# Residual with a matrix per subject on one core: the subjects' numbers and the weights loaded by another engine, in other row counts

## The chip, the cores and the metric

One core of a Trainium2 chip runs the whole program. The metric is the device time of one execution in microseconds; three executions of the kernel before gave 323.35, 324.01 and 324.10 us (median 324.01).

## The reference

There are 128 samples of 128 x 1024 f32 (`x`, indices b, c, t), a number 0 to 7 for each sample (`subjects`) and 8 matrices of 128 x 128 f32 (`weights`). The output is the input plus a product with the sample's own matrix:

```python
w = weights[subjects]
out = x + jnp.einsum('bct,bcd->bdt', x, w)
```

So 64 MB are read, 64 MB written, and each sample takes one 128 x 128 by 128 x 1024 product in f32.

## The kernel before, in words

A tile is two samples, one on partitions 0 to 63 and one on 64 to 127; each partition holds two neighbouring rows of a sample (8 KB). There are 64 tiles. Tiles travel in pairs: one load brings two tiles (2 MB). `x_ring` has 12 slots, so room for 6 pairs, and a result is written over its own input before it is stored from there.

SP (line 88 on) issues the load of the weights first (line 90: 128 partitions, 4 KB each in four pieces of 1 KB), then the 32 loads of x (line 98). The loads of pairs 4 and 5 wait for the landing of pairs 0 and 1. From pair 6 on each load waits until everything stored from its slots has landed (`x_out`, line 95). ACT (line 171 on) issues the load of the subjects' numbers, the same 128 numbers on 16 partitions (line 190), although only partition 0 is read, and all stores (lines 202 and 205): single tiles for the first two and the last four, pairs for the rest. Thus there are two hardware queues in use, and the order inside each is the program's order. Nothing but `x_ring`'s slots ties loads to stores.

Before the first product, DVE clamps the subjects' numbers (line 144). Then DVE and ACT wait for the weights and rearrange them into `weight_bank` (lines 113 and 174), each two copies of 64 x 1024. POOL has made an identity (`eye`, lines 102 and 106), which DVE adds (line 119), so that the product brings part of the residual with it. DVE loads numbers into registers (line 124) and copies the matrices of four tiles into `weight_ring` (line 132, "pick"). TensorE then does 16 matmuls and 16 weight loads per tile (line 222); DVE adds x to two quarters of the products (lines 139 and 140), ACT copies the other two (lines 182 and 183), and ACT issues the store.

Of the kernel before, what the change touches and what calls it, by code (L numbers as in the profile page):

```python
# [6 lines left out]
DMA_INC = 16  # L7
# [7 lines left out]
def subject_residual_kernel(nc, x, subjects, weights, out):  # L15
# [9 lines left out]
    f32, i32 = mybir.dt.float32, mybir.dt.int32  # L25
    B, C, T = x.shape
    S, _, D = weights.shape
    assert C == D == nc.NUM_PARTITIONS
    H, R = C // 2, 2
# [6 lines left out]

    SINGLE = (*range(PAIR), *range(TILES - REST, TILES))

    SUBJECT_ROWS = 16

    def stores(pairs, place):

        return sum(PAIR if (pair * PAIR_SLOTS + place) * PAIR in SINGLE else 1 for pair in range(pairs))
# [3 lines left out]
    EVENS, ODDS = slice(0, S, 2), slice(1, S, 2)  # L47
    add = mybir.AluOpType.add

    x_of_pair = x.rearrange("(n j a) (h r) t -> n (a h) j (r t)", j=PAIR, a=2, r=R)  # L50
    out_of_pair = out.rearrange("(n j a) (h r) t -> n (a h) j (r t)", j=PAIR, a=2, r=R)

    with ExitStack() as ctx:  # L53
        x_ring = ctx.enter_context(nc.sbuf_tensor("x_ring", [C, SLOTS, R, T], f32))

        weight_halves = ctx.enter_context(nc.sbuf_tensor("weight_halves", [C, S // 2, R, D], f32))
# [3 lines left out]

        eye = ctx.enter_context(nc.sbuf_tensor("eye", [C, H], f32))
        subject_row = ctx.enter_context(nc.sbuf_tensor("subject_row", [SUBJECT_ROWS, B], i32))
        product = [[ctx.enter_context(nc.psum_tensor(f"product{i}_{a}", [D, T], f32)) for a in range(2)]
                   for i in range(PRODUCTS)]

        subjects_in = ctx.enter_context(nc.semaphore("subjects_in"))
        clamped = ctx.enter_context(nc.semaphore("clamped"))
        weights_in = ctx.enter_context(nc.semaphore("weights_in"))
        eye_zero = ctx.enter_context(nc.semaphore("eye_zero"))
        eye_low = ctx.enter_context(nc.semaphore("eye_low"))  # L70
        eye_high = ctx.enter_context(nc.semaphore("eye_high"))
# [15 lines left out]

        @block.sync
        def _(sp):
            sp.dma_start(weight_halves[:, :, :, :],  # L90
                         weights.rearrange("(i a) (h r) d -> (a h) i (r d)", a=2, r=R)).then_inc(weights_in, DMA_INC)
            for pair in range(PAIRS):
                lap, place = divmod(pair, PAIR_SLOTS)
                if lap:
                    sp.wait_ge(x_out[place], stores(lap, place) * DMA_INC)
                elif place >= LOADS_AHEAD:
                    sp.wait_ge(x_in[place - LOADS_AHEAD], DMA_INC)
                sp.dma_start(x_ring[:, place * PAIR:(place + 1) * PAIR, :, :], x_of_pair[pair]).then_inc(x_in[place], DMA_INC)

        @block.gpsimd  # L100
        def _(pool):
            pool.memset(eye[:, :], 0.0).then_inc(eye_zero, 1)  # L102
            pool.wait_ge(eye_zero, 1)
            for begin, made in ((0, eye_low), (H, eye_high)):
                half = slice(begin, begin + H)
                pool.affine_select(eye[half, :], eye[half, :], pattern=[[-1, H]], base=0, channel_multiplier=1,  # L106
                                   compare_op=mybir.AluOpType.not_equal, fill=1.0).then_inc(made, 1)

        @block.vector
        def _(dve):  # L110
            def bank(half, source, subjects_of):

                return dve.tensor_copy(  # L113
                    weight_bank[half, subjects_of, :, :].rearrange("h i r (q k) -> h i r q k", q=2),
                    weight_halves[source, :, :, :].rearrange("h i r (k q) -> h i r q k", q=2))

            def add_eye(half, row, columns):
                cells = weight_bank[half, :, row, columns]
                return dve.tensor_tensor(cells, cells, eye[half, :].rearrange("h (s k) -> h s k", s=1).broadcast_to(  # L119
                    (H, S, H)), add)  # L120

            def subjects_of(tile):

                _, numbers = nc.values_load_multi_w_load_instructions(  # L124
                    subject_row[0:1, tile * 2:(tile + PICK_AHEAD) * 2], engines=(mybir.EngineType.DVE,), min_val=0,
                    max_val=S - 1, skip_runtime_bounds_check_because="DVE has clamped subject_row to 0 .. S - 1")
                return numbers

            def pick(slot, numbers):

                for subject, half in zip(numbers, (LOW, HIGH)):
                    done = dve.tensor_copy(weight_ring[half, slot, :, :], weight_bank[half, bass.ds(subject, 1), :, :])  # L132
                return done

            def sums(tile, slot):

                low, high = product[slot % PRODUCTS]
                dve.wait_ge(multiplied, tile + 1)
                dve.tensor_tensor(x_ring[LOW, slot, 0, :], low[LOW, :], x_ring[LOW, slot, 0, :], add)  # L139
                dve.tensor_tensor(x_ring[HIGH, slot, 1, :], high[HIGH, :], x_ring[HIGH, slot, 1, :], add).then_inc(summed, 1)  # L140

            dve.sem_inc(summed, PRODUCTS)
            dve.wait_ge(subjects_in, DMA_INC)
            dve.tensor_scalar(subject_row[0:1, :], subject_row[0:1, :], 0, S - 1, mybir.AluOpType.max,  # L144
                              mybir.AluOpType.min).then_inc(clamped, 1)
            dve.wait_ge(weights_in, DMA_INC)
            bank(LOW, LOW, EVENS)
            bank(LOW, HIGH, ODDS).then_inc(bank_low, 1)
            dve.wait_ge(eye_low, 1)
            dve.wait_ge(bank_low, 1)  # L150
            add_eye(LOW, 1, ODD)
            dve.wait_ge(eye_high, 1)
            dve.wait_ge(bank_high, 1)  # L153
            add_eye(HIGH, 0, EVEN).then_inc(eyes_added, 1)
            dve.wait_ge(eyes_added, 1)
            dve.wait_ge(clamped, 1)
            numbers = subjects_of(0)
            for tile in range(PICK_AHEAD):
                pick(tile, numbers[tile * 2:tile * 2 + 2]).then_inc(picked, 1)


            for tile in range(TILES):
                sums(tile, tile % SLOTS)
                ahead = tile + PICK_AHEAD
                if ahead < TILES:
                    if ahead % PICK_AHEAD == 0:
                        numbers = subjects_of(ahead)
                    own = ahead % PICK_AHEAD * 2
                    pick(ahead % SLOTS, numbers[own:own + 2])

        @block.scalar
        def _(act):
            def bank(half, source, subjects_of):
                return act.copy(  # L174
                    weight_bank[half, subjects_of, :, :].rearrange("h i r (q k) -> h i r q k", q=2),
                    weight_halves[source, :, :, :].rearrange("h i r (k q) -> h i r q k", q=2))

            def cross(tile, slot):

                low, high = product[slot % PRODUCTS]  # L180
                act.wait_ge(multiplied, tile + 1)
                act.copy(x_ring[LOW, slot, 1, :], low[HIGH, :])  # L182
                act.copy(x_ring[HIGH, slot, 0, :], high[LOW, :]).then_inc(copied, 1)  # L183

            def whole(tile):

                act.wait_ge(copied, tile + (PRODUCTS + 1))
                act.wait_ge(summed, tile + (PRODUCTS + 1))  # L188

            act.dma_start(subject_row[:, :], subjects.rearrange("(one b) -> one b", one=1).broadcast_to(  # L190
                (SUBJECT_ROWS, B))).then_inc(subjects_in, DMA_INC)
            act.sem_inc(copied, PRODUCTS)
            act.wait_ge(weights_in, DMA_INC)
            bank(HIGH, LOW, EVENS)
            bank(HIGH, HIGH, ODDS).then_inc(bank_high, 1)
            for tile in range(TILES):
                slot = tile % SLOTS
                place, j = divmod(slot, PAIR)
                cross(tile, slot)
                if tile in SINGLE:  # L200
                    whole(tile)
                    act.dma_start(out_of_pair[tile // PAIR, :, j, :], x_ring[:, slot, :, :]).then_inc(x_out[place], DMA_INC)
                elif j == PAIR - 1:
                    whole(tile)
                    act.dma_start(out_of_pair[tile // PAIR], x_ring[:, place * PAIR:(place + 1) * PAIR, :, :]).then_inc(
                        x_out[place], DMA_INC)
            for place in reversed(range(PAIR_SLOTS)):
                act.wait_ge(x_out[place], DMA_INC * stores(LAPS + (place < REST // PAIR), place))
# [39 lines left out]
```

## Time and profile before

| What | before |
|---|---|
| span of the profiled execution | 321.5 us |
| time of that same execution | 323.31 us (1.8 us lie outside the span) |
| median of three executions | 324.01 us |
| data moved | 134.83 MB, mean 419 GB/s over the span |
| PE / DVE / ACT / POOL busy | 76% / 61% / 41% / 0% |
| queue q1 (SP's), queue q10 (ACT's) | 50.2% and 49.4% of the 16 DMA engines' span |

How to read it: "DMA share" is the mean busy share of the 16 DMA engines. Packets are booked at rounded durations, so a full stretch can read 1.01. A share of 0.31 means that about 5 of 16 engines have work. A landing time runs from the issue of a transfer to the moment at which all of it has arrived.

### The profile page before, as it was taken

To read this page: it belongs to the slowest core of one execution; us is meant where nothing else is said; L and a number is where in the kernel's file an instruction comes from. 1 tells how busy PE (TensorE), PEld (TensorE's weight loads), DVE (VectorE), ACT (ScalarE), POOL (GpSimd) and SP (SyncE) were. 2 spreads that over 40 slices of the span, in tenths; PEclk is the share of its full clock that TensorE was granted. 3 is DMA by queue.
4 is the path that set the end of the run, shared out by engine and by line. 5 is a ranking of instruction groups with operands and counts; after the bars stand their busy time and mean duration, and the time that the engine had idled before them with its cause. 6 is when DMAs were issued, how large, how long until landed. Compare 5 with 4: busy or idle time off the path is not lost.

```text
span 321.5 us, 2871 instructions
## 1 busy us (share of the span) xinstructions
PE 243.8 (76%) x1024; PEld 112.7 (35%) x1024; DVE 196.3 (61%) x261; ACT 132.2 (41%) x131; POOL 0.8 (0%) x7
## 2 busy tenths in 40 slices
PE   0799997878687866779868698666986868876650
PEld 0344442334343432334424244333333434443320
DVE  3288888637657555764757737567463774755560
ACT  4056566324444242542425525335342553443450
POOL 1000000000000000000000000000000000000000
PEclk9999999979989997997979979998897998999995
DMA  7999999999999999999999999999999999999996
GB/s 287 422 411 427 421 428 425 428 429 429 425 428 428 428 426 428 428 427 427 428 429 428 426 427 430 428 425 428 430 427 426 426 431 428 426 425 432 421 428 271
DMA packets 18024, 134.83 MB, mean 419 GB/s; under 512 B 1105, under 2 KB 1633, under 8 KB 1633
## 3 DMA queue, kind: packets, MB, share of 16 engines
q1 hardware_dynamic: 9232, 67.64, 50.2%
q10 hardware_dynamic: 8784, 67.12, 49.4%
q8 instruction: 2, 0.03, 0.0%
q14 instruction: 6, 0.04, 0.0%
HBM read 67.64 MB, written 67.11 MB: 419 GB/s over the span
## 4 chain that ended last, share of the span: by engine, by line
DMA 73%; PE 17%; DVE 3%; issue 3%; DVEq 1%; ACT 1%; ACTq 0%
DMA out<-x_ring 37%; DMA x_ring<-x 34%; PE product L222 17%; DVE x_ring L140 2%; DMA weight_halves<-weights 1%; ACT weight_bank L174 1%; DVE x_ring L139 1%; DVEq L53 0%; DVEq L124 0%; DVEq L132 0%; DVE weight_bank L119 0%; DVE weight_ring L132 0%; ACTq L188 0%; DVEq L153 0%
## 5 line engine op out<-in xcount | busy, mean ns | idle before, releaser
L222 PE MATMUL product<-x_ring,weight_ring 64*128 64x512 f32 x1024 | 243.8, 630 | 66.1 <-DMA x_ring<-x 43.2
L222 PEld LDWEIGHTS product<-x_ring,weight_ring 64*128 64x128 f32 x1024 | 112.7, 199 | 196.4 <-issue 123.2
L139 DVE TENSOR_TENSOR x_ring<-product,x_ring 64x1024 f32<-64x1024 f32 x64 | 77.9, 1217 | 106.6 <-PE product L222 106.6
L182 ACT COPY x_ring<-product 64x1024 f32<-64x1024 f32 x64 | 64.5, 1008 | 175.5 <-PE product L222 175.5
L140 DVE TENSOR_TENSOR x_ring<-product,x_ring 64x1024 f32<-64x1024 f32 x64 | 78.6, 1228 | 0.8
L183 ACT COPY x_ring<-product 64x1024 f32<-64x1024 f32 x64 | 64.2, 1003 | 0.8
L132 DVE COPY weight_ring<-weight_bank 64x256 f32 x128 | 36.9, 288 | 3.9 <-issue 1.0
L174 ACT COPY weight_bank<-weight_halves 64x1024 f32<-64x1024 f32 x2 | 2.2, 1115 | 2.1 <-DMA weight_halves<-weights 2.1
L144 DVE TENSOR_SCALAR subject_row<-subject_row 1x128 int32<-1x128 int32 x1 | 0.2, 215 | 3.6 <-DMA subject_row<-subjects 3.6
L113 DVE COPY weight_bank<-weight_halves 64x1024 f32<-64x1024 f32 x2 | 1.4, 688 | 0.9 <-DMA weight_halves<-weights 0.9
L174 ACT ACT_TABLE_LOAD x1 | 1.3, 1283 | 1.3 <-PEq L240 1.3
L119 DVE TENSOR_TENSOR weight_bank<-weight_bank,eye 64x512 f32<-64x512 f32 x2 | 1.4, 686 | 0.3 <-ACT weight_bank L174 0.2
L106 POOL TENSOR_SCALAR_AFFINE_SELECT eye<-eye 64x64 f32<-64x64 f32 x2 | 0.5, 234 | 0.3 <-POOL eye L102 0.2
L102 POOL MEMSET eye<- 128x64 f32 x1 | 0.2, 151 | 0.3 <-POOLq L240 0.3
L240 POOL MEMSET const-float32-0.0<- 128x1 f32 x1 | 0.1, 98 | 0.2 <-issue 0.2
L240 POOL MEMSET const-float32-1.0<- 128x1 f32 x1 | 0.1, 98 | 0.0
L240 POOL MEMSET const-bfloat16-1.0<- 128x1 bf16 x1 | 0.1, 98 | 0.0
L240 POOL MEMSET const-uint8-127<- 128x1 uint8 x1 | 0.1, 98 | 0.0
## 6 DMA issues: line engine op xcount, KB each, us to landing
x_ring<-x SPq DMA_DIRECT2D x32, 2048.0 KB, 22.0
out<-x_ring ACTq DMA_DIRECT2D x29, 2048.0 KB, 26.2
out<-x_ring ACTq DMA_DIRECT2D x6, 1024.0 KB, 10.6
weight_halves<-weights SPq DMA_DIRECT2D x1, 512.0 KB, 3.9
subject_row<-subjects ACTq DMA_DIRECT2D x1, 8.0 KB, 2.8
```

Of the source, the lines that this page charges most:

```text
L102: pool.memset(eye[:, :], 0.0).then_inc(eye_zero, 1)
L106: pool.affine_select(eye[half, :], eye[half, :], pattern=[[-1, H]], base=0, channel_multiplier=1, compare_op=mybir.AluOpType.not_equal, fi ...
L113: return dve.tensor_copy(weight_bank[half, subjects_of, :, :].rearrange("h i r (q k) -> h i r q k", q=2), weight_halves[source, :, :, :].r ...
L119: return dve.tensor_tensor(cells, cells, eye[half, :].rearrange("h (s k) -> h s k", s=1).broadcast_to((H, S, H)), add)
L132: done = dve.tensor_copy(weight_ring[half, slot, :, :], weight_bank[half, bass.ds(subject, 1), :, :])
L139: dve.tensor_tensor(x_ring[LOW, slot, 0, :], low[LOW, :], x_ring[LOW, slot, 0, :], add)
L140: dve.tensor_tensor(x_ring[HIGH, slot, 1, :], high[HIGH, :], x_ring[HIGH, slot, 1, :], add).then_inc(summed, 1)
L174: return act.copy(weight_bank[half, subjects_of, :, :].rearrange("h i r (q k) -> h i r q k", q=2), weight_halves[source, :, :, :].rearrang ...
L182: act.copy(x_ring[LOW, slot, 1, :], low[HIGH, :])
L183: act.copy(x_ring[HIGH, slot, 0, :], high[LOW, :]).then_inc(copied, 1)
L222: last = pe.matmul(product[slot % PRODUCTS][a][:, cols], weight_ring[half, slot, r, :], x_ring[half, slot, r, cols], start=r == 0, stop=r ...
L240: nc = bacc.Bacc("TRN2", target_bir_lowering=False, num_devices=1)
```

## The change

SP now loads only the weights of the last two partitions, and signals that on a semaphore of its own. POOL, which issued no transfer before, first loads the subjects' numbers to 5 partitions, then the weights of the other 126 partitions, then the subjects' numbers once more to 13 partitions of a new tensor `last_row` that nothing reads; only then does it make `eye`, and at its end it waits for the last of the three. ACT issues no load any more. DVE and ACT wait for both parts of the weights.

```diff
-    SUBJECT_ROWS = 16
+    SUBJECT_ROWS, WEIGHT_ROWS, LAST_ROWS = 5, 126, 13
...
+    weights_of_partition = weights.rearrange("(i a) (h r) d -> (a h) i (r d)", a=2, r=R)
...
+        last_row = ctx.enter_context(nc.sbuf_tensor("last_row", [LAST_ROWS, B], i32))
...
         @block.sync
         def _(sp):
-            sp.dma_start(weight_halves[:, :, :, :],
-                         weights.rearrange("(i a) (h r) d -> (a h) i (r d)", a=2, r=R)).then_inc(weights_in, DMA_INC)
+            sp.dma_start(weight_halves[WEIGHT_ROWS:, :, :, :].rearrange("p i r d -> p i (r d)"),
+                         weights_of_partition[WEIGHT_ROWS:]).then_inc(more_weights_in, DMA_INC)
...
         @block.gpsimd
         def _(pool):
+            def row(rows):
+                return subjects.rearrange("(one b) -> one b", one=1).broadcast_to((rows, B))
+
+            pool.dma_start(subject_row[:, :], row(SUBJECT_ROWS)).then_inc(subjects_in, DMA_INC)
+            pool.dma_start(weight_halves[0:WEIGHT_ROWS, :, :, :].rearrange("p i r d -> p i (r d)"),
+                           weights_of_partition[0:WEIGHT_ROWS]).then_inc(weights_in, DMA_INC)
+            pool.dma_start(last_row[:, :], row(LAST_ROWS)).then_inc(last_in, DMA_INC)
             pool.memset(eye[:, :], 0.0).then_inc(eye_zero, 1)
...
+            pool.wait_ge(last_in, DMA_INC)
...
             dve.wait_ge(weights_in, DMA_INC)
+            dve.wait_ge(more_weights_in, DMA_INC)
...
-            act.dma_start(subject_row[:, :], subjects.rearrange("(one b) -> one b", one=1).broadcast_to(
-                (SUBJECT_ROWS, B))).then_inc(subjects_in, DMA_INC)
             act.sem_inc(copied, PRODUCTS)
             act.wait_ge(weights_in, DMA_INC)
+            act.wait_ge(more_weights_in, DMA_INC)
```

## Rows read from the trace of the kernel before

**Rows 1.** The page: DMA share and GB/s in 40 slices, then the queues.

```profile
DMA  7999999999999999999999999999999999999996
GB/s 287 422 411 427 421 428 425 428 429 429 425 428 428 428 426 428 428 427 427 428 429 428 426 427 430 428 425 428 430 427 426 426 431 428 426 425 432 421 428 271
...
q8 instruction: 2, 0.03, 0.0%
q14 instruction: 6, 0.04, 0.0%
```

**Rows 2.** Stretches: length, busy of each engine, PEclk, DMA share, GB/s.

```profile
0.00:1.75 1.75, 0.00 (x0) 0.00 (x0) 0.00 (x0) 0.46 (x1) 0.82 (x7) 1.00 0.00 0
1.75:3.95 2.20, 0.00 (x0) 0.00 (x0) 0.21 (x1) 0.82 (x1) 0.00 (x0) 1.00 0.92 240
4.00:34.00 30.00, 23.61 (x100) 10.70 (x102) 20.50 (x33) 12.63 (x13) 0.00 (x0) 1.00 1.01 422
60.00:280.00 220.00, 174.40 (x722) 81.07 (x718) 135.74 (x180) 90.51 (x90) 0.00 (x0) 0.93 1.01 428
```

**Rows 3.** The same for stretches at the very end.

```profile
317.50:318.00 0.50, 0.00 (x0) 0.00 (x0) 0.00 (x0) 0.00 (x0) 0.00 (x0) 0.50 1.01 426
...
318.50:319.00 0.50, 0.00 (x0) 0.00 (x0) 0.00 (x0) 0.00 (x0) 0.00 (x0) 0.50 0.31 131
...
319.50:319.75 0.25, 0.00 (x0) 0.00 (x0) 0.00 (x0) 0.00 (x0) 0.00 (x0) 0.50 0.16 66
...
320.25:320.50 0.25, 0.00 (x0) 0.00 (x0) 0.00 (x0) 0.00 (x0) 0.00 (x0) 0.50 0.08 33
320.50:320.75 0.25, 0.00 (x0) 0.00 (x0) 0.00 (x0) 0.00 (x0) 0.00 (x0) 0.50 0.00 0
```

**Rows 4.** Queues from 35 to 38 us: packets, MB, share of 16 engines.

```profile
q10 hardware_dynamic: 76, 0.62, 49.8%
q1 hardware_dynamic: 82, 0.61, 49.7%
q8 instruction: 1, 0.02, 1.9%
q14 instruction: 1, 0.01, 0.6%
```

**Rows 5.** Timeline, 0 to 12 us: start, us, engine, line, operation.

```profile
0.73 0.42 SPq L90 DMA_DIRECT2D weight_halves<-weights  x1
0.74 0.44 ACTq L190 DMA_DIRECT2D subject_row<-subjects  x1
1.12 0.53 POOL L106 TENSOR_SCALAR_AFFINE_SELECT eye<-eye 64x64 f32<-64x64 f32 x2 [0.24 <-POOL eye L102]
1.21 8.81 SPq L98 DMA_DIRECT2D x_ring<-x  x5
3.59 0.21 DVE L144 TENSOR_SCALAR subject_row<-subject_row 1x128 int32<-1x128 int32 x1 [3.59 <-DMA subject_row<-subjects]
4.69 1.39 DVE L113 COPY weight_bank<-weight_halves 64x1024 f32<-64x1024 f32 x2 [0.88 <-DMA weight_halves<-weights]
6.19 0.68 DVE L119 TENSOR_TENSOR weight_bank<-weight_bank,eye 64x512 f32<-64x512 f32 x1
10.39 2.08 PE L222 MATMUL product<-x_ring,weight_ring 64*128 64x512 f32 x4 [10.39 <-DVE weight_ring L132]
```

**Rows 6.** ACT's timeline, 0 to 45 us: the first three stores.

```profile
19.04 0.37 ACTq L202 DMA_DIRECT2D out<-x_ring  x1
...
22.46 0.34 ACTq L202 DMA_DIRECT2D out<-x_ring  x1
...
29.33 0.39 ACTq L205 DMA_DIRECT2D out<-x_ring  x1
```

**Rows 7.** The chain that ended last, 0 to 56 us.

```profile
0.73 3.93 DMA weight_halves<-weights
...
22.46 11.51 DMA out<-x_ring
33.99 22.30 DMA x_ring<-x
```

**Rows 8.** The page: landing time of the subjects' numbers.

```profile
subject_row<-subjects ACTq DMA_DIRECT2D x1, 8.0 KB, 2.8
```

**Rows 9.** Timeline near the end: the last store.

```profile
312.48 0.34 ACTq L202 DMA_DIRECT2D out<-x_ring  x1
```

More of the change, by code:

```diff
@@ L67, in subject_residual_kernel @@
         clamped = ctx.enter_context(nc.semaphore("clamped"))
+        last_in = ctx.enter_context(nc.semaphore("last_in"))
         weights_in = ctx.enter_context(nc.semaphore("weights_in"))
+        more_weights_in = ctx.enter_context(nc.semaphore("more_weights_in"))
         eye_zero = ctx.enter_context(nc.semaphore("eye_zero"))
```

## Prediction

> **What bounds the kernel now.** I read the page's slices first. The DMA row stands at 9 in every slice but the first and the last, at 411 to 432 GB/s between them, so the 16 DMA engines are the bound and the kernel is a stream of bytes [rows 1]. I then read the ends in stretches. Nothing moves before 1.75 us; from 60 to 280 us the rate is 428 GB/s, that is 26.75 GB/s or 0.306 us per 8 KB piece for each engine [rows 2]. At the other end the stream doesn't stop at once. Until 318.0 all engines are busy; from 318.5 to 319.0 the share is 0.31, which is 5 engines of 16; from 319.5 on the bytes are those of about two engines (66 GB/s, then 33; a piece is booked where it starts, and 33 GB/s over 0.25 us is one piece); the last piece starts between 320.25 and 320.5, and with its 0.306 us ends near 320.6 [rows 3]. So 11 engines are done at about 318.2, three near 319.6, and two near 320.5. The time is set by the two last engines, not by the mean: about 2.3 us, or 0.7%, lie between most engines and the last.
>
> Where may a late engine come from? The queues from 35 to 38 us show code being loaded by the same engines: one packet of q8 takes 1.9% of 16 engines' 3 us, 0.91 us of one engine, and one of q14 0.6%, 0.29 us [rows 4]. The whole execution has two and six such packets [rows 1]. Three engines late by about 1.4 us and two by more fit a few such hits each; nothing in the queries says which engines by number.
>
> The start of the arithmetic is another matter: the weights land 3.93 us after their issue, and the first matmul comes at 10.39 [rows 5, 7]. That delays no byte, because x is loaded ahead meanwhile.
>
> **The change, part by part.** The sum is made against the profiled execution, 323.31 us with its span of 321.5; the median of the runs is 324.01, 0.70 above it.
>
> *SP's queue.* The load of the weights takes 0.42 us of SP's time at 0.73, and x follows at 1.21 [rows 5]. A load for two partitions takes its place, so x is issued at 1.1 to 1.21; no later than before, for a smaller transfer in the same position. First bytes appeared at about 1.8, so 1.1 us after the issue [rows 2, 5]. Before, the engines had weights to move from 1.8; now 14 or more of them wait until x arrives, at about 2.3. The stream starts later by 0 to 0.48 us; I take +0.48, since x's own place is hardly moved.
>
> *The weights' bytes.* From 1.75 to 3.95 us, 240 GB/s x 2.2 = 528 KB were moved: the 524 KB of weights and hardly more [rows 2]. At 428 GB/s they would take 1.22 us; they took some 2.15. Now they are moved among the pieces of x. If only their bytes count, 0.93 us of each engine is saved; if the 0.9 us is the price of 1 KB pieces or of any first transfer, nothing is. I take the middle, -0.55. If the 126 partitions are spread over 14 engines, each of these moves 36 pieces of 1 KB and not 32: an eighth of 1.2 to 2.15 us, +0.15 to +0.27, I take +0.19. The sum for an ordinary engine: 0.48 - 0.55 + 0.19 = +0.12, between 0 - 0.93 + 0 = -0.93 and 0.48 + 0 + 0.27 = +0.75.
>
> *The subjects' numbers.* 8 KB before, 2.5 and 6.5 KB now; 1 KB more in a stream of 134.83 MB is nothing. Their landing took 2.8 us from ACT [rows 8]. From POOL it may take as long or several us more. DVE's clamp at 3.59 sat 0.9 us before the copies of the weights, which now come later too [rows 5]. ACT loses an issue of 0.44 us and gains no time by it: it waits for the weights anyway.
>
> *The start of the arithmetic.* Here a wait grows. The weights go to POOL's queue behind one small transfer. No row shows POOL issuing; the nearest are 0.42 and 0.44 us for an issue on SP and ACT, and a landing 3.93 us after it [rows 5, 7]. The low end of the delay D is therefore 0.4 us (one issue ahead). At the high end each 1 KB piece of an engine waits for an 8 KB piece of x: 36 x (0.306 + 0.05) = 12.8 us from about 3.3, landing near 16.1 instead of 4.66, D = 11.4. (0.05 is an estimate: 2.15 us over 32 pieces gives 0.067, 1.22 over 32 gives 0.038.) Behind the wait stand DVE's and ACT's copies, the identity, the pick, and then TensorE, whose first matmul would be at 10.39 + D. I take D near 5.
>
> What hides D is the ring. It takes six pairs, 12.6 MB, 29.8 us of loading at 422 GB/s, from about 3.95 to 33.8 without a store [rows 2]. Stores of two tiles add 5 us, so with the first two stores queued the engines have work until 38.8. The third store, issued at 29.33 + D with its first bytes 1.1 us later, must be there by then: D below 8.4. Or the seventh load is, which waits for the first two stores: it came at 33.99 before [rows 6, 7]. So D = 5 costs nothing. Afterwards TensorE and the rest catch up, since PE is busy 174 of 220 us [rows 2]. At the end the last store was issued at 312.48, with 1.1 us to its first bytes, while the last 1 MB needs only the 2.5 us before 318.2: some 2 us of room, and a late start of the stores lets loads run ahead, which widens it [rows 9].
>
> *POOL.* `eye` is made at 0.7 to 1.65 and needed at 6.19 [rows 5]; behind three issues it may be 2 to 5 us later, but the copies before its use move by D too. The final wait for 13 rows is over some 300 us before the end.
>
> *The sum.* +0.12 for every engine, and for the late ones too if they are still given weights: 323.43 for the profiled execution, 324.13 beside the median; I say 324.1.
>
> **Rivals.**
>
> *A. That sum:* no change, the late engines stay late. 324.1, its own range 323.2 to 324.8.
>
> *B. The late engines are spared.* 126 is not a multiple of 16 and 14 x 9 is 126. If the transfer runs on 14 engines, two move no weights and save 1.2 to 2.15 us against the others. If these are the two that end near 320.5, they end at 320.5 + 0.48 - 2.15 = 318.8 to 320.5 + 0.48 - 1.22 = 319.8, and the three at 319.6 + 0.12 = 319.7 decide: -0.8 from 320.5, with -1.7 and -0.1 as bounds (the low one where ordinary engines too gain their full 0.93). That gives 323.2. For it: two engines do stand apart from the rest at the end [rows 3]. Against it: no row says which engines these are, and if just one of them is spared the other ends the kernel as before. The Trainium skill, "DMA: Bandwidth & Descriptors", section "Why a DMA increments its semaphore by 16 and not by 1", says that a transfer runs on the largest number of engines up to 16 that divides its slowest dimension, the lowest-numbered ones from SP, and from the GpSimd side consecutive ones from a cursor that moves on; by that rule 5, 126 and 13 rows take 5, 14 and 13 engines, 32 in all, so that the cursor is back where it was, the two spared engines are the same in each execution, and SP's two rows fall on engines 0 and 1. The same section has an exception by which some such transfers take all 16 with fewer rows for the last, and then B does not occur. No row of this trace shows POOL's queue.
>
> *C. The ring runs dry: slower.* If each 1 KB piece queues behind an 8 KB piece, and POOL takes 2 us or more to produce the descriptors, D passes 12. From D = 8.4 the engines wait up to 1.1 us for the seventh load's first bytes, once; from 22.46 + D + 1.1 = 36.3, D = 12.7, also for the second store, 1 us for each us of D. At D = 13 that is 1.1 + 0.3, and 0.12 to 0.48 of the start: +1.5 to +1.9, 325.7. It decides once the weights land later than about 17 us. For it: packets of q1 and q10 alternate evenly whenever both have work, 49.7 to 49.8% [rows 4]. Against it: 12 us of delay are a lot beside a landing of 3.93. The same page's section "SWDGE vs HWDGE vs iDMA" says that an engine changes its queue only at packet boundaries and that a packet holds up to about 4096 bytes of descriptors; by that a partition's four pieces pass together, 9 turns of 0.306 + 0.2 us instead of 36, 4.6 us, and D is near 3, which speaks against C.
>
> *D. It doesn't do what it says.* POOL's transfer runs on 16 engines with 8 rows each and 6 for the last; the sum is then A's without 0.19: 324.0.
>
> **How the numbers follow.** A 0.44, B 0.34, C 0.17, D 0.05. A difference under 0.3%, 0.97 us, is not told from none here; the bound applies to the three chances. B passes it in some 6 of 10 of its cases (0.20), A's low end adds 0.05: faster 0.25. C gives 0.15, A's high end with a little scatter 0.10: slower 0.25. Same 0.50. The range leaves out the low tail of B and the high tail of C: 322.7 to 325.8.
>
> **What would show each step.** The first bytes near 2.3 us, not 1.8, and x's first pair landing a little earlier than before confirm SP's part. The landing of `weight_halves<-weights` from POOL gives D; the first matmul should be at 10.39 + D, and no stretch from 30 to 50 us below a DMA share of 1.00. A gap there is C. The staircase at the end decides between A and B: in A the share is still 0.31 for over 1 us and the last bytes come 2.3 us after the first engines stop; in B the last step, that of the two engines, is gone. The forecast is wrong if the time outside the span grows with a third queue, if POOL's queue slows the stream beyond the start, or if the last store comes after 315.

## The result, and the profile after

The changed kernel takes 326.10 us (median of 7 executions, 325.11 to 326.56); the kernel before took 324.07 us beside it (median of 7, 323.35 to 324.80). The ratio is 1.0061 with a 95% interval of 1.0048 to 1.0074: it became 2.0 us slower. The forecast was 324.1 us and no change. The profiled execution took 325.16 us with a span of 323.3, 1.85 us above the profiled one of before, and still 1.9 us outside the span.

The timeline of the changed kernel from 0 to 24 us (start, us, engine, line, operation) shows the new order of the start:

```profile
0.74 0.34 SPq L97 DMA_DIRECT2D weight_halves<-weights  x1
1.13 15.39 SPq L105 DMA_DIRECT2D x_ring<-x  x6
1.24 0.68 POOL L112 DMA_DIRECT2D subject_row<-subjects  x1 [0.80 <-POOLq L255]
1.91 0.88 POOL L113 DMA_DIRECT2D weight_halves<-weights  x1
7.11 0.21 DVE L159 TENSOR_SCALAR subject_row<-subject_row 1x128 int32<-1x128 int32 x1 [7.11 <-DMA subject_row<-subjects]
12.39 1.39 DVE L128 COPY weight_bank<-weight_halves 64x1024 f32<-64x1024 f32 x2 [5.06 <-DMA weight_halves<-weights]
18.13 6.35 PE L237 MATMUL product<-x_ring,weight_ring 64*128 64x512 f32 x18 [18.13 <-DVE weight_ring L147]
```

The weights are issued at 1.91 and land 10.5 us later, so the copies start at 12.39 and the first matmul at 18.13 instead of 10.39 [rows 5]: a delay D of 7.7 us. The larger part of it is a wait for the first byte: from 4 to 6 us POOL's queue (q0) moves four packets and 0.00 MB, so the rows of the weights pass only from about 6 us on.

```profile
q1 hardware_dynamic: 104, 0.85, 101.3%
q0 software_dynamic: 4, 0.00, 0.3%
```

What this did to the stream is seen in stretches (length, busy of each engine, PEclk, DMA share, GB/s). First the kernel after, then the kernel before in stretches that [rows 2] do not have:

```profile
1.75:4.00 2.25, 0.00 (x0) 0.00 (x0) 0.00 (x0) 1.28 (x1) 1.94 (x6) 1.00 0.78 202
4.00:6.00 2.00, 0.00 (x0) 0.00 (x0) 0.00 (x0) 0.00 (x0) 0.24 (x1) 1.00 1.02 427
6.00:12.00 6.00, 0.00 (x0) 0.00 (x0) 0.21 (x1) 0.00 (x0) 0.00 (x0) 1.00 1.02 341
12.00:34.00 22.00, 15.87 (x64) 7.17 (x66) 14.08 (x24) 8.29 (x8) 0.00 (x0) 1.00 1.01 422
34.00:60.00 26.00, 26.00 (x124) 11.69 (x122) 22.75 (x31) 15.65 (x16) 0.00 (x0) 1.00 1.01 425
280.00:314.00 34.00, 24.80 (x96) 11.82 (x96) 17.85 (x20) 13.10 (x14) 0.00 (x0) 0.88 1.01 427
```

```profile
1.75:4.00 2.25, 0.00 (x0) 0.00 (x0) 0.21 (x1) 0.82 (x1) 0.00 (x0) 1.00 0.94 252
4.00:6.00 2.00, 0.00 (x0) 0.00 (x0) 1.30 (x2) 1.30 (x2) 0.00 (x0) 1.00 1.02 429
6.00:12.00 6.00, 1.61 (x4) 0.85 (x6) 3.76 (x11) 0.93 (x1) 0.00 (x0) 1.00 1.01 425
12.00:34.00 22.00, 22.00 (x98) 9.85 (x96) 15.45 (x21) 10.40 (x11) 0.00 (x0) 1.00 1.01 420
34.00:60.00 26.00, 23.87 (x114) 10.56 (x112) 20.79 (x28) 13.73 (x14) 0.00 (x0) 1.00 1.01 425
```

The loss sits in two rows. From 1.75 to 4 us, (252 - 202) x 2.25 / 428 = 0.26 us of stream are missing. From 6 to 12 us, (425 - 341) x 6 / 428 = 1.18 us are missing, and in that row the DMA share is 1.02: the engines are busy all the time and move a fifth less. Everything behind it is level: 422 against 420, 425 against 425, and 428 in the long middle as in [rows 2]. Together 1.44 us.

The packets and queues from 6 to 12 us (packets, MB, share of 16 engines), after and then the queue before, tell what was slow:

```profile
DMA packets 400, 2.04 MB, mean 341 GB/s; under 512 B 81, under 2 KB 88, under 8 KB 214
...
q1 hardware_dynamic: 202, 1.52, 76.1%
q0 software_dynamic: 198, 0.52, 25.7%
```

```profile
q1 hardware_dynamic: 327, 2.55, 101.1%
```

Six microseconds of 16 engines are 96 us. An 8 KB piece of x took 1.011 x 96 / (2.55 MB / 8192) = 0.31 us before. After, it took 0.761 x 96 / (1.52 MB / 8192) = 0.39 us while POOL's weights (q0) passed. 214 - 88 = 126 packets lie between 2 and 8 KB: one of 4 KB for each row of the weights. Such a row took 0.257 x 96 / (0.52 MB / 4096) = 0.19 us.

At the end the stairs of [rows 3] are still there, later. The kernel after:

```profile
318.00:319.00 1.00, 0.00 (x0) 0.00 (x0) 0.00 (x0) 0.00 (x0) 0.00 (x0) 0.50 1.08 459
319.00:319.50 0.50, 0.00 (x0) 0.00 (x0) 0.00 (x0) 0.00 (x0) 0.00 (x0) 0.50 0.74 311
319.50:320.00 0.50, 0.00 (x0) 0.00 (x0) 0.00 (x0) 0.00 (x0) 0.00 (x0) 0.50 0.36 148
321.50:321.75 0.25, 0.00 (x0) 0.00 (x0) 0.00 (x0) 0.00 (x0) 0.00 (x0) 0.50 0.15 66
322.00:322.25 0.25, 0.00 (x0) 0.00 (x0) 0.00 (x0) 0.00 (x0) 0.00 (x0) 0.50 0.08 33
```

Most engines stop near 319.6 instead of 318.2, five or so go on, two are still at work at 321.5, and the last piece starts after 322.0 (before: after 320.25). So most engines are 1.4 us later and the last one 1.7 to 1.8. The further 0.3 us is on the last engine; a code packet was longer, 2.4% of 48 us = 1.15 us from 43 to 46 us where [rows 4] had 0.91, but that it fell on this very engine no row shows.

### The profile page after: what moved, and what is told of

The parts are those of the page before. It is cut to its first block, busy times and chain, and to the rows that moved or that the text cites. A ratio compares the mean times of both kernels' runs of the same rounds, so it can differ in the third digit from the quotient of the medians.

```text
span 323.3 us, 2876 instructions
## 1 busy us (share of the span) xinstructions
PE 243.1 (75%) x1024; PEld 112.5 (35%) x1024; DVE 196.3 (61%) x261; ACT 132.4 (41%) x131; POOL 2.9 (1%) x10
## 4 chain that ended last, share of the span: by engine, by line
DMA 63%; PE 27%; DVE 2%; issue 2%; DVEq 1%; ACT 1%; POOL 0%; ACTq 0%; POOLq 0%
DMA out<-x_ring 40%; PE product L237 27%; DMA x_ring<-x 20%; DMA weight_halves<-weights 3%; DVE x_ring L155 2%; ACT weight_bank L190 1%; DVE x_ring L154 0%; DVEq L56 0%; DVEq L139 0%; DVE weight_bank L134 0%; DVE weight_ring L147 0%; POOL subject_row L112 0%; DVEq L147 0%; ACTq L204 0%; DVEq L169 0%
## 5 line engine op out<-in xcount | busy, mean ns | idle before, releaser
L113 POOL DMA_DIRECT2D weight_halves<-weights x1 | 0.9, 877 | 0.0
L112 POOL DMA_DIRECT2D subject_row<-subjects x1 | 0.7, 675 | 0.8 <-POOLq L255 0.8
## 6 DMA issues: line engine op xcount, KB each, us to landing
out<-x_ring ACTq DMA_DIRECT2D x6, 1024.0 KB, 10.5
weight_halves<-weights POOLq DMA_DIRECT2D x1, 504.0 KB, 10.5
```

Of the source, the lines that this page charges most:

```text
L112: pool.dma_start(subject_row[:, :], row(SUBJECT_ROWS)).then_inc(subjects_in, DMA_INC)
L113: pool.dma_start(weight_halves[0:WEIGHT_ROWS, :, :, :].rearrange("p i r d -> p i (r d)"), weights_of_partition[0:WEIGHT_ROWS]).then_inc(we ...
```

## The experiments

Four theories stood after the result. 1: POOL's pieces and those of x slow one another. 2: any second queue beside x does. 3: the way in which the weights are cut into rows costs, either (3a) because engines write partitions that others write at that time, or (3b) because 14 engines carry what 16 did. No trace here says which engine writes which partition, so 3a and 3b speak of a spread that is inferred from the row counts. 4: the late start of the arithmetic costs. Each run is compared with the kernel before on the same chip; differences in us are taken from the ratio.

**All 128 rows by POOL.**

```diff
-            sp.dma_start(weight_halves[:, :, :, :], ...)
...
+            pool.dma_start(subject_row[:, :], ...)       # 16 partitions, no third load
+            pool.dma_start(weight_halves[:, :, :, :].rearrange("p i r d -> p i (r d)"), ...)
```

> POOL loads the numbers to 16 partitions and the weights of all 128, nothing is loaded to 13 partitions, SP loads only x. Theory 1 (POOL's pieces and the pieces of x slow one another while they pass together; 366, 318 and 337 GB/s in three stretches of 2 us after 6 us in the changed kernel, against 428): the same loss without the uneven spread, 1.2 us from the mingling and 0.3 from the later start, so +1.2 to +2.0 us against the kernel before. Theory 2 (any transfer on a second queue beside x does this): the same. Theory 3 (the uneven spread over 14 engines is what costs): within 0.5 us of the kernel before. Theory 4 (the late start of the arithmetic costs): +1.5 to +2.0, with stretches of a DMA share under 1.00 at 30 to 50 us.

Measured: 323.65 us against 324.06, ratio 0.9996 (0.9987 to 1.0005). No loss. Its first stretch, then the stretch and the queues from 6 to 12 us:

```profile
1.75:4.00 2.25, 0.00 (x0) 0.00 (x0) 0.00 (x0) 0.35 (x1) 1.56 (x5) 1.00 0.93 251
6.00:12.00 6.00, 0.00 (x0) 0.00 (x0) 0.93 (x3) 0.73 (x1) 0.00 (x0) 1.00 1.02 414
...
q1 hardware_dynamic: 255, 1.96, 80.0%
q0 software_dynamic: 158, 0.53, 22.1%
```

The weights still come through POOL beside x, yet the rate is 414 and not 341. By the same arithmetic a piece of x takes 0.32 us and a row of weights 0.16. Its first matmul comes at 17.01, D = 6.6. Theories 1 and 2, and theory 4 up to this D, expected +1.2 us or more and are refuted; theory 3 expected this. The first row tells something else: with x alone in it the stretch from 1.75 to 4 us has 251 GB/s, and with the weights in front the kernel before has 252. The slow first 2 us are therefore the price of whatever is moved first, not of 1 KB pieces.

**126 and 2 rows by SP, ahead of x.**

```diff
+            sp.dma_start(weight_halves[0:126], weights_of_partition[0:126]).then_inc(weights_in, DMA_INC)
+            sp.dma_start(weight_halves[126:], weights_of_partition[126:]).then_inc(more_weights_in, DMA_INC)
```

> The kernel before, but SP loads the weights in two transfers, 126 partitions and 2, both ahead of x; ACT loads the numbers. The uneven spread without POOL and without mingling. Theories 1, 2 and 4: no loss, within 0.6 us of the kernel before, first matmul within 1 us of 10.39; if two late engines happen to be spared, up to -0.8. Theory 3: +1 to +2 us.

Measured: 324.79 against 324.06, ratio 1.0017 (1.0007 to 1.0027), +0.55 us. Neither size was right. The stretch in which the last weights meet the first x is slow here too (429 in the kernel before):

```profile
4.00:6.00 2.00, 0.00 (x0) 0.00 (x0) 0.48 (x1) 0.51 (x1) 0.00 (x0) 1.00 1.02 340
```

(429 - 340) x 2 / 428 = 0.42 us. So 126 rows slow the stream without POOL too, over the short time that they overlap with x. How much of the +0.55 us is theirs is open: the profiled execution is the slowest of twelve (325.42), and in it the last store was issued at 316.56 (312.48 before, [rows 9]) and engines were without work near the end:

```profile
316.00:317.00 1.00, 0.00 (x0) 0.00 (x0) 0.47 (x1) 0.04 (x1) 0.00 (x0) 0.77 0.57 238
```

The first matmul was at 12.49, partly because ACT loaded its table only when the weights had landed.

**The weights by ACT's hardware queue, beside x.**

```diff
+            act.dma_start(weight_halves[:, :, :, :], ...).then_inc(weights_in, DMA_INC)   # behind the numbers
```

> The kernel before, but ACT's hardware queue takes the load of the weights, behind the numbers, beside x on SP's. Mingling without POOL. Theory 1 (POOL's queue is needed for the loss): at most +0.5 us, pieces of x keep near 0.31 us while the weights pass, 420 GB/s or more from 4 to 12 us. Theory 2 (any second queue): +1.2 to +1.7 us with about 340 GB/s while they pass. Theory 4 (late arithmetic): the weights come in single 1 KB pieces and land at 10 us or later, so as much as the changed kernel or more, +2.

Measured: 327.49 against 324.06, ratio 1.0103 (1.0088 to 1.0117), +3.3 us. While the weights pass the rate is full, 422 GB/s from 6 to 12 us, so theory 2 is wrong; theory 1 had the rate right and the time (at most +0.5 us) wrong, and theory 4 expected late weights and the loss. The weights pass in single 1 KB pieces that alternate with pieces of x, 288 and 289 packets in these 6 us, and land 16.1 us after their issue; the first matmul is at 23.01, D = 12.6. The loss comes later, where the ring has run dry:

```profile
6.00:12.00 6.00, 0.00 (x0) 0.00 (x0) 0.00 (x0) 0.00 (x0) 0.00 (x0) 1.00 1.02 422
...
q1 hardware_dynamic: 289, 2.24, 88.5%
q10 hardware_dynamic: 288, 0.29, 13.9%
...
34.00:40.00 6.00, 6.00 (x30) 2.70 (x28) 5.17 (x9) 3.17 (x4) 0.00 (x0) 1.00 0.82 343
40.00:44.00 4.00, 4.00 (x22) 1.85 (x20) 3.58 (x5) 2.58 (x3) 0.00 (x0) 1.00 0.74 252
44.00:48.00 4.00, 4.00 (x22) 1.81 (x20) 3.57 (x6) 2.57 (x4) 0.00 (x0) 1.00 0.98 311
```

Here the DMA share falls, to 0.82 and 0.74: engines without work, unlike the row of the changed kernel at 1.02 with few bytes. That is (1.01 - 0.82) x 6 + (1.01 - 0.74) x 4 = 2.2 us without work. Behind it stands a row with nearly full share and 311 GB/s, though no weights pass any more: (425 - 311) x 4 / 428 = 1.07 us lost by slow pieces. Both are what theory 4 looks like, and at 34 to 60 us the changed kernel, at 425 GB/s, shows neither.

**POOL loads only the numbers.**

```diff
-            pool.dma_start(weight_halves[0:WEIGHT_ROWS], ...)      # SP loads all 128 rows, as before
```

> The changed kernel, but SP loads all 128 partitions of the weights as before; POOL only loads the numbers to 5 and to 13 partitions. Theory 1: 9 KB cost nothing, within 0.4 us of the kernel before. Rival (a third queue in use costs by itself, outside the span or in it): +1.5 to +2 us. Theory 4: the numbers land at 7 us at the latest, so the first matmul is at most 1 us later and no loss.

Measured: 324.18 against 324.06, ratio 1.0004 (0.9995 to 1.0012). A third queue and 9 KB through it cost nothing. The numbers landed 5.7 us after their issue (2.8 from ACT, [rows 8]) and moved the first matmul to 12.61, 2.2 us later and not "at most 1"; that too was free.

**64 and 64 rows by POOL.**

```diff
+            pool.dma_start(weight_halves[LOW], weights_of_partition[LOW]).then_inc(weights_in, DMA_INC)
+            pool.dma_start(weight_halves[HIGH], weights_of_partition[HIGH]).then_inc(more_weights_in, DMA_INC)
```

> POOL loads the numbers to 16 partitions and the weights in two transfers of 64 partitions each; SP loads only x. Every DMA engine gets the same bytes (4 rows of each transfer), but an engine's rows are no longer the partitions that it writes in a transfer of 128 partitions. Theory 3a (what costs is that some engines then write partitions that x's pieces go to through other engines): the rate falls under 380 GB/s while the weights pass beside x, and the kernel loses 0.8 to 1.6 us like the changed one. Theory 3b (what costs is that 14 engines carry what 16 carried): no loss, within 0.4 us of the kernel before, as with one transfer of 128. Theory 1 (POOL's pieces beside x): already against the run with 128 partitions, which was level; no loss.

Measured: 327.62 against 323.58, ratio 1.0108 (1.0090 to 1.0126), +3.5 us by the ratio. This is the run that parts 3a from 3b: 64 rows can be spread evenly over 16 engines, and the loss is larger than in the changed kernel. Its stretches and queues:

```profile
6.00:12.00 6.00, 0.00 (x0) 0.00 (x0) 0.21 (x1) 0.00 (x0) 0.00 (x0) 1.00 1.05 301
...
q1 hardware_dynamic: 173, 1.29, 75.7%
q0 software_dynamic: 165, 0.52, 28.9%
...
34.00:60.00 26.00, 26.00 (x124) 11.62 (x122) 22.98 (x30) 15.92 (x16) 0.00 (x0) 1.00 0.99 389
40.00:44.00 4.00, 4.00 (x22) 1.83 (x20) 3.54 (x7) 2.01 (x2) 0.00 (x0) 1.00 0.91 377
44.00:48.00 4.00, 4.00 (x20) 1.73 (x18) 3.23 (x6) 2.16 (x3) 0.00 (x0) 1.00 0.99 317
48.00:52.00 4.00, 4.00 (x22) 1.80 (x20) 3.59 (x5) 2.58 (x3) 0.00 (x0) 1.00 0.99 338
```

A piece of x takes 0.46 us, a row of weights 0.22. (425 - 301) x 6 / 428 = 1.74 us are lost there, about half of the whole. The rest is from 34 to 60 us, (425 - 389) x 26 / 428 = 2.2 us: the first matmul came at 20.43, D = 10.0, and the ring ran dry at 40 us. But only the row from 40 to 44 us has a low share; it loses 0.45 us. From 44 to 52 us the share is 0.99 and 1.8 us are lost all the same: a piece of 8 KB takes 0.99 x 64 / 155 = 0.41 us from 44 to 48 us, long after the last weights. The row behind the gap in the run by ACT's queue is slow in the same way. So in both runs a gap was followed by some microseconds of slow pieces; why is open.

**64 and 64 rows by SP, ahead of x.**

```diff
+            sp.dma_start(weight_halves[0:64], weights_of_partition[0:64]).then_inc(weights_in, DMA_INC)
+            sp.dma_start(weight_halves[64:], weights_of_partition[64:]).then_inc(more_weights_in, DMA_INC)
```

> The kernel before, but SP loads the weights as 64 and 64 partitions, both ahead of x; the numbers come by ACT. The same question without POOL and with nearly no x beside the weights. Theory 3a: a small loss, 0.3 to 0.7 us, with a rate under 380 GB/s between 3 and 6 us, since half of the engines write one half's partitions twice over. Theory 3b: no loss.

Measured: 325.47 against 323.58, ratio 1.0052 (1.0034 to 1.0070), +1.7 us, above the 0.3 to 0.7 of theory 3a. Most of it stands in the first rows:

```profile
1.75:4.00 2.25, 0.00 (x0) 0.00 (x0) 0.21 (x1) 0.00 (x0) 0.00 (x0) 1.00 0.75 181
4.00:6.00 2.00, 0.00 (x0) 0.00 (x0) 0.17 (x1) 0.20 (x1) 0.00 (x0) 1.00 0.86 226
6.00:12.00 6.00, 0.00 (x0) 0.00 (x0) 3.40 (x7) 3.29 (x3) 0.00 (x0) 1.00 0.99 401
```

(252 - 181) x 2.25 / 428 + (429 - 226) x 2 / 428 + (425 - 401) x 6 / 428 = 0.37 + 0.95 + 0.34 = 1.66 us, about the +1.7. (The profiled execution, at 325.97 us, lost more: from 12 to 34 us it had 412 GB/s against 420, another 0.41 us.) The shares of 0.75 and 0.86 say that a part of the first two is engines without work: SP issued x at 2.15 us here, not at 1.21, behind two issues of 0.70 and 0.60 us. So this run does not give the price of the row cut by itself.

**Two column halves of all 128 rows by POOL: the control.**

```diff
+            pool.dma_start(weight_halves[:, 0:2], weights_of_partition[:, 0:2, :]).then_inc(weights_in, DMA_INC)
+            pool.dma_start(weight_halves[:, 2:4], weights_of_partition[:, 2:4, :]).then_inc(more_weights_in, DMA_INC)
```

> As the kernel with two transfers of 64 partitions by POOL, but each of the two now takes all 128 partitions and half of the matrices (2 KB a partition). Two transfers by POOL, the same bytes, but each engine's rows are those it writes in x's loads. Theory 3a (what costs is writing partitions that other engines write at that time): over 405 GB/s from 6 to 12 us and within 0.5 us of the kernel before. Rival (two transfers by POOL cost what was seen): near 300 GB/s from 6 to 12 us and +3 us.

Measured: 324.79 against 324.04, ratio 1.0024 (1.0009 to 1.0038), +0.8 us where 0.5 was the limit, against +3.5 for 64 and 64.

Packets and POOL's queue from 1.75 to 13 us, then two stretches:

```profile
DMA packets 670, 4.32 MB, mean 384 GB/s; under 512 B 64, under 2 KB 80, under 8 KB 208
q0 software_dynamic: 192, 0.53, 12.1%
...
6.00:12.00 6.00, 0.00 (x0) 0.00 (x0) 0.81 (x2) 0.62 (x1) 0.00 (x0) 1.00 1.02 414
...
34.00:60.00 26.00, 26.00 (x124) 11.57 (x122) 23.10 (x30) 16.05 (x16) 0.00 (x0) 1.00 1.01 421
```

414 GB/s: two transfers by POOL slow the stream as little as one when each takes all 128 partitions. The run with 64 and 64 rows by POOL has these packets in the same time:

```profile
DMA packets 579, 3.57 MB, mean 318 GB/s; under 512 B 64, under 2 KB 80, under 8 KB 208
q0 software_dynamic: 192, 0.53, 15.9%
```

In both, POOL's queue moves 192 packets and 0.53 MB, and 208 - 80 = 128 packets lie between 2 and 8 KB. Neither the number nor the size of POOL's packets makes the difference between 414 and 301 GB/s; which partitions each transfer goes to does.

The 0.8 us is open. The first matmul is at 18.35, D = 8.0, and (425 - 421) x 26 / 428 = 0.24 us are missing from 34 to 60 us, so the late arithmetic may be a part. But the profiled execution took 323.88 us, less than the median of the kernel before, and its rows can't show what made the others slower.

**Other engines spared.**

```diff
-    SUBJECT_ROWS, WEIGHT_ROWS, LAST_ROWS = 5, 126, 13
+    SUBJECT_ROWS, WEIGHT_ROWS, LAST_ROWS = 16, 126, 2     # and 9, 126, 9
```

> The changed kernel with 16, 126 and 2 rows instead of 5, 126 and 13: POOL's 14 engines start elsewhere, so other engines are spared. Theory 3a and 3b: a loss of 1 to 2 us all the same, somewhat different under 3a since other partitions collide. Rival (the loss is where it is because the late engines of the kernel before were not among the spared): if now they are, the last bytes come at most 1.5 us after the first engines stop, not 2.9, and the loss shrinks to under 1 us.

> The changed kernel with 9, 126 and 9 rows: a third place for the 14 engines. Expected as for 16, 126 and 2; the two runs together show how much the time depends on which engines are spared. Theory 3a and 3b: +1 to +2 us. Rival (which engines are spared decides): one of these differs from the changed kernel by more than 1 us.

Measured: 325.84 and 325.78 against 323.58, ratios 1.0062 (1.0047 to 1.0077) and 1.0071 (1.0056 to 1.0085); the changed kernel's is 1.0061. From 6 to 12 us:

```profile
6.00:12.00 6.00, 0.00 (x0) 0.00 (x0) 0.22 (x1) 0.00 (x0) 0.00 (x0) 1.00 1.03 336
```

```profile
6.00:12.00 6.00, 0.00 (x0) 0.00 (x0) 0.21 (x1) 0.00 (x0) 0.00 (x0) 1.00 1.02 338
```

The first is of 16, 126, 2. The row counts around the 126 don't matter, within what can be measured. In none of the three is the last step of the stairs gone: the last piece starts after 322.0 in the changed kernel, after 323.0 with 16, 126 and 2 rows, and after 322.5 with 9, 126 and 9.

**SP's two rows behind the first x.**

```diff
             for pair in range(PAIRS):
...
                 sp.dma_start(x_ring[...], x_of_pair[pair]).then_inc(x_in[place], DMA_INC)
+                if pair == 0:
+                    sp.dma_start(weight_halves[WEIGHT_ROWS:], ...).then_inc(more_weights_in, DMA_INC)
```

> The changed kernel, but SP issues the two rows of weights behind the first load of x, so x is issued at 0.74 and not at 1.13. All theories: the first bytes of x come 0.35 us earlier and the stream is ahead by 0.2 to 0.35 us at 6 us, with the loss of 1.2 us from 6 to 12 us unchanged, so the time is 0.2 to 0.4 us below the changed kernel, +1.4 to +1.9 us against the kernel before. Rival (the small transfer itself disturbs the stream's start): more than 0.6 us below.

Measured: 325.62 against 324.04, ratio 1.0049 (1.0035 to 1.0064), or +1.6 us, inside its expected +1.4 to +1.9. The steps behind it missed. From 1.75 to 4 us there are 226 GB/s instead of 202, which is 0.13 us and not 0.2 to 0.35. And the row from 6 to 12 us, expected unchanged, lost (425 - 325) x 6 / 428 = 1.40 us:

```profile
6.00:12.00 6.00, 0.00 (x0) 0.00 (x0) 0.22 (x1) 0.50 (x1) 0.00 (x0) 1.00 1.02 325
```

The intervals of this kernel and the changed one overlap, so the times show no gain from the earlier x.

## Why the prediction was wrong

*The step that failed* is "The weights' bytes": the weights moved among the pieces of x were put at -0.55 us, between -0.93 and 0, plus 0.19 for 14 engines. Measured against the kernel before, the stretch in which they pass costs +1.18 us. The bound of "nothing is saved" was taken as the worst case; that one transfer can slow another was not priced at all. The sum for an ordinary engine, +0.12 with +0.75 as its top, came out at +1.44. The prediction's own sign of being wrong, "if POOL's queue slows the stream beyond the start", is the one that came.

*The gain that was booked* did not exist either. The prediction left open whether the 0.9 us between 1.22 and 2.15 was the price of 1 KB pieces or of any first transfer. The run with 128 rows by POOL answers it: 251 GB/s from 1.75 to 4 us with x alone, 252 with the weights in front. It is the price of whatever is moved first. (The middle of -0.93 and 0 would also have been -0.47, not -0.55; that changes nothing here.)

*What is in its place.* What decides is not POOL (128 rows by POOL: 414 GB/s and 0.9996), nor the second queue (422 GB/s), nor the number or size of the packets (192 on POOL's queue in both runs with two transfers), but how the weights are cut by partitions (column halves of 128 rows: 414; row halves: 301; 126 rows: 325 to 341). Where the cut is harmful, the pieces of both transfers take longer and the share stays full, for about five microseconds. That much is shown by these pairs of runs. That engines then write partitions which x's loads write through other engines is the explanation that fits; no trace names an engine or a partition, so it stays inferred, and by what mechanism two engines would hinder one another no row shows. That 14 engines carry what 16 did (3b) is not needed for a loss, as 64 rows show; whether it adds anything at 126 was not tested.

The Trainium skill has a mechanism, "SBUF — State Buffer", section "Door 1: The DMA port swizzle (why `[64,N]` ≈ `[32,N]`)": 16 ports, each serving eight fixed partitions, of which partitions 0 to 63 reach only eight. The low rates of 64 and 64 rows, 301 GB/s by POOL and 226 by SP against 425 and 429, agree with it in direction. And the Trainium skill's "DMA: Bandwidth & Descriptors", section "The descriptor swizzle", says that in a transfer of 128 partitions each engine writes one port, which the level runs with 128 rows agree with.

*The start.* First bytes were put later by 0.48 us at no more than that price; the stretch from 1.75 to 4 us lost 0.26. Right within its size, as part of a term that was netted against the wrong gain.

*D and the ring.* D was taken as 5 between 0.4 and 11.4; it is 7.7. The prediction let the weights' pieces pass from about 3.3 us on; they passed from about 6. The threshold of 8.4 below which it is free held in direction: D = 6.6 cost nothing, 7.7 nothing in the profiled execution, 8.0 at most a little, and with 10.0 and 12.6 there was a gap. Beyond the threshold it is dearer than rival C said (+1.5 to +1.9 at D = 13, +3.3 us measured at 12.6): the gap itself was 2.2 us without work where C had 1.4, and C had nothing for the slow pieces behind it, 1.07 us from 44 to 48 us, and 1.8 us at D = 10.0.

*Rival A* did not hold: the late engines stayed late, as it said, but the rest of its sum did not. *Rival B*, that two late engines are spared: its gain did not appear with any of three row counts. *Rival C* gave the nearest time, 325.7, by a mechanism that did not occur at this D: no gap, a share of 1.01 from 34 to 60 us. The argument held against it, that a row of the weights passes as one piece, was right: 126 packets of 4 KB. *Rival D* gave 324.0, which is not the time. But whether POOL's 126 rows went over 14 engines or over 16, with six for the last, no row shows: the run with 128 rows is another cut. Two engines without weights should be 9 x 0.19 = 1.7 us ahead of the others; the full share of 1.08 from 318 to 319 us gives no sign that any had stopped, while most stopped near 319.6. So two such engines are not seen at the end; they could only be among the late ones.

*Late engines.* The prediction said that a few code packets each fit the lateness. They don't: three engines late by 1.4 us and two by 2.3 are 8.8 us, and all eight packets of [rows 1] together, at 0.91 and 0.29 us, are 3.6. What makes these engines late is open.

*What stays open.* The medians differ by 2.0 us, the profiled executions by 1.85, of which 1.44 are in rows; the 0.3 on the last engine may in part be the longer code packet.

## What to carry to other kernels

When a stream saturates the DMA engines, a small transfer beside it is not priced by its bytes alone: look at its row count. With all 128 partitions it cost little more than its bytes here; cut to 126 or 64 rows and issued by POOL, the same half megabyte cost 1.2 to 1.7 us more of the whole stream. A DMA share of 1.0 does not mean full speed; read the GB/s beside it, and separate rows with a full share and few bytes (slow pieces) from rows with a low share (no work). And a delay ahead of the first product is free as long as the ring has loads queued, here up to about 8 us; once the ring runs dry, count more than the gap, for the pieces behind it were slow as well.

## What was not expected of the hardware

With a transfer of 126 partitions issued by POOL beside the loads of x, the pieces of both took longer: 8 KB pieces from 0.31 to 0.39 us and 4 KB rows from 0.16 to 0.19; with 64-partition transfers 0.46 and 0.22. POOL's transfers landed late for their size: 2.5 KB 5.8 us after the issue, against 2.8 us for 8 KB from ACT. After the gap with 64 and 64 rows by POOL, 8 KB pieces took 0.41 us instead of 0.31 from 44 to 48 us, with a share of 0.99. And the two kinds of queue shared the engines differently: through POOL a partition's four 1 KB pieces went as one 4 KB packet and the weights landed in 9.3 us (128 rows), through ACT's hardware queue each 1 KB waited its turn and they took 16.1 us.
